# Routed layers with one block up to the experts, expert regions of fixed place, and attention operands merged with combination and normalisation

## The chip, the cores and the metric

One core of a Trainium2 chip runs one program. Its engines work side by side, each on its own instruction stream, and meet in semaphores: TensorE (PE, with its weight loads PEld), VectorE (DVE), ScalarE (ACT), GpSimd (POOL) and SyncE (SP), which issues most transfers. The metric is the device time in microseconds (us), median over runs.

## The reference

The input x has 2 x 1024 tokens of 256 values, the context 2 x 77 tokens. Four layers follow each other, each an attention and a feed-forward part with a residual sum:

```
x = x + L0_attention(norm(x), ctx);      x = x + L0_ffn(norm(x))       # causal, with mixed scores; quantised ffn
x = x + L1_attention(ctx, norm(x));      x = x + L1_ffn(norm(x))       # latent attention; ROUTED ffn, ReLU, capacity 320
x = x + L2_attention(norm(x), ctx);      x = x + L2_ffn(norm(x))       # cross attention; gated mixture of all experts
x = x + L3_attention(norm(x), ctx);      x = x + L3_ffn(norm(x))       # cross attention with a bias; ROUTED ffn, GELU, biases
```

A routed part chooses one of 8 experts for each token and computes only that one:

```
probs = softmax(norm(x) @ gate_w);  e = argmax(probs)            # per token, 8 experts
y = act(norm(x) @ w1[e] + b1[e]) @ w2[e] + b2[e]                 # 256 -> 1024 -> 256
x = x + probs[e] * y          # in L1 only for the first 320 tokens of an expert
```

A cross attention takes queries from the normalised tokens and keys and values from the context (16 heads of 16 values, 77 keys).

## The kernel before

Every stage is one or more blocks. In a block each engine has its own instruction list; a block ends when all engines have ended theirs, and the next begins. A `Stage` clears its semaphores in a block of its own when it is left. x stays in SBUF as `env.x` (16 tiles of 128 tokens), with its statistics in `env.stats`.

**Routed layer** (`routed_ffn_stage`, tags m1 and m3). `route_tokens` first issues two weight loads of 8 MB (lines 3007, 3008) and runs `layernorm_stage`: VectorE normalises 16 tiles, TensorE turns them and multiplies by the gate, ScalarE copies. A second block takes the logits of all 16 tiles at once: VectorE finds the expert of every token, TensorE counts, VectorE works out `slot`, a place in a dense list in which each expert's tokens are padded to whole tiles of 128 (`NT` = 23 tiles). GpSimd then scatters 16 tiles of rows into `sorted_x` in DRAM (line 3050, one indirect transfer a tile), which was filled with zeros in the first stage (line 754).

`routed_experts` runs over the 23 tiles. `tiles` writes out two, loops over 18, two in a turn, and writes out three. For tile j (buffer u = j % 2):

- SyncE loads the rows of a tile as soon as its buffer is free, up to two tiles ahead (line 3162).
- TensorE (`work`): `expand(j+1)`, the first product; `turn_x(j+2)`, turning of the rows; `reduce(j)`, the second product.
- VectorE: `copy_w(j+2)`, the weights of that tile's expert into `w_mine`; `keep_x(j+2)`; then the copy of the output of tile j (line 3259 or 3261).
- GpSimd stores that output to `sorted_y` (line 3170).

All engines that need the expert of a tile read its number from `expert_of` with `value_load`. TensorE and VectorE wait at the start for all weights. `combine_experts` gathers rows from `sorted_y` by `slot` (GpSimd, line 3290), VectorE adds them (3297) and takes statistics (3301).

**Cross attention** (`cross_attention_stage`, tags c2 and c3). `cross_operands` runs `layernorm_stage`, then a block of its own: loads of the weights, context turned, keys, values, the largest value over all partitions (GpSimd, line 3407), then all queries (line 3433). `cross_attend` follows.

**Latent attention** (`latent_attend`, tag lta, once for each b). For each of 16 heads and 9 key tiles TensorE scores, ScalarE takes exponentials (line 2858), VectorE and GpSimd split them into two halves, TensorE weighs. SyncE stages queries, keys and values of the next head while one is worked on.

Of the kernel before, what the change touches and what calls it, by code (L numbers as in the profile page):

```python
# [7 lines left out]
ALU = mybir.AluOpType  # L8
# [301 lines left out]
class Env:  # L310


    def __init__(self, nc, ctx):
# [8 lines left out]
        self.sorted_x = [nc.dram_tensor(f"sorted_x{k}", [NT * P, D], F32).ap() for k in range(2)]  # L322
# [4 lines left out]
        self.stored = sems("expert_rows_stored", 2)  # L327
# [343 lines left out]
def project_qkv(nc, env, st, ctx, args, name, kern_dram, q_dram, k_dram, near_dram, mixed_dram, vals, edges, size, mask, other):  # L671
# [70 lines left out]
    def _(sp):  # L742
# [1829 lines left out]
def latent_attend(nc, env, st, ctx, b, p, qT, kT, v16, v32):  # L2572
# [35 lines left out]
    TURN = 3  # L2608

# [215 lines left out]
    def _(act):  # L2825
# [20 lines left out]
        for h in range(H):  # L2846
            for j in range(KT):
# [112 lines left out]
NT = T // P + E - 1  # L2960


def routed_ffn_stage(nc, env, tag, args, name, func, biased, capacity, out=None):
# [6 lines left out]
    sorted_x, zero_stored = env.sorted_x.pop(0), env.zero_stored.pop(0)  # L2970
    sorted_y = nc.dram_tensor(f"{tag}_sorted_y", [NT * P, D], F32).ap()
    with ExitStack() as ctx:
# [5 lines left out]
        slot = st.sb("slot", [P, TILES], U32)  # L2978
        weight = st.sb("weight", [P, TILES])
        expert_of = st.sb("expert_of", [P, NT], I32)  # L2980
        weights_loaded = st.sem("weights_loaded")
        with ExitStack() as inner:
            route_tokens(nc, env, Stage(nc, inner, tag + "r"), inner, tag, w, capacity, sorted_x, zero_stored, slot, weight,
                         expert_of, w1, w2, b1, b2, weights_loaded)
        with ExitStack() as inner:
            routed_experts(nc, env, Stage(nc, inner, tag + "e"), inner, func, sorted_x, sorted_y, expert_of, w1, w2, b1, b2,
                    weights_loaded)
        with ExitStack() as inner:  # L2988
            combine_experts(nc, env, Stage(nc, inner, tag + "c"), inner, sorted_y, slot, weight, out)


def route_tokens(nc, env, st, ctx, tag, w, capacity, sorted_x, zero_stored, slot, weight, expert_of, w1, w2, b1, b2, weights_loaded):

    xn = st.sb("xn", [P, TILES, D])
    xnT = st.sb("xnT", [P, DC, T])
    gate = st.sb("gate", [P, DC, E])
    gate_loaded = st.sem("gate_loaded")
    b1_rows = st.sb("b1_rows", [E * FC, P])
    rows_loaded, b1_turned, b1_kept = (st.sem(n) for n in ("rows_loaded", "b1_turned", "b1_kept"))

    def load(sp):

        sp.dma_start(gate[:], w("gate_w").rearrange("(c p) e -> p c e", p=P)).then_inc(gate_loaded, 16)
        if b1 is not None:
            sp.dma_start(b1_rows[:], w("b1").rearrange("e (c p) -> (e c) p", p=P)).then_inc(rows_loaded, 16)
            sp.dma_start(b2[:], w("b2").partition_broadcast(P)).then_inc(weights_loaded, 16)
# [3 lines left out]
    lg_ps, lg_done = st.ps("lg_ps", [P, 512]), st.sem("lg_done")  # L3010
    layernorm_stage(nc, env, tag + "l", env.x, dst_tok=xn, dst_T=xnT, ahead=load,
                    gates=(gate, gate_loaded, 16, lg_ps, lg_done))
    upto, all_ones = st.sb("upto", [P, P], BF16), st.sb("all_ones", [P, P], BF16)
    lower = st.sb("lower", [P, E, E])
    ids = st.sb("ids", [P, E])
    tile_ids = st.sb("tile_ids", [P, NT])
# [254 lines left out]
def combine_experts(nc, env, st, ctx, sorted_y, slot, weight, out):  # L3271
# [22 lines left out]
    def _(dve):  # L3294
# [8 lines left out]
        if out is None:  # L3303
            dve.wait_ge(summed, TILES)
# [820 lines left out]
```

## Time and profile before

| | us |
|---|---|
| median of 3 runs | 3418.19 (3417.17 to 3421.18) |
| profiled execution, its own time | 3417.33 |
| its span | 3415.7 |
| TensorE / VectorE / ScalarE / GpSimd busy | 2921.4 / 2085.7 / 1895.5 / 1302.8 |
| first routed layer | about 1847 to 2080 |
| combination and operands of the second cross attention | about 2082 to 2142 |
| operands of the last attention | about 2987 to 3022 |
| second routed layer with combination | about 3152 to the end |

The span is that of the profiled execution from its first to its last instruction; stages follow each other, so a place in it names a stage. In a timeline row stand start, duration, engine, line, what is written from what, and in brackets the idle time before it with what ended it. `x16` or `x32` means that so many instructions are merged in a row.

### The profile page before, as it was taken

The numbers are of one execution on the slowest core, as the hardware profiler recorded it, in microseconds if no ns is written. First come the engines' busy times: TensorE is split into PE (matmuls) and PEld (weight loads), VectorE is DVE, ScalarE is ACT, GpSimd is POOL, SyncE is SP. The second block draws the span as 40 slices with busy tenths as digits, with TensorE's granted clock in tenths as the row PEclk, the third lists the DMA queues.
The fourth block names the chain that finished last, engine by engine and source line by source line (L and its number), as shares of the span: only waits on it lengthen the run. The fifth ranks groups of instructions, "written<-read, shape, count | busy, mean of one in ns | idle before, by whom it ended". The sixth has DMA issues, their size and how long they took to land. (4 is left out here: it accounts for less than half of the span.)

```text
span 3415.7 us, 68343 instructions
## 1 busy us (share of the span) xinstructions
PE 2921.4 (86%) x26674; PEld 2033.7 (60%) x26675; DVE 2085.7 (61%) x3098; ACT 1895.5 (55%) x2864; POOL 1302.8 (38%) x942
## 2 busy tenths in 40 slices
PE   6779998737879998889997695979999999988596
PEld 3246665415446666456666694766666666667595
DVE  6968887587867873877873224855444444466122
ACT  3448886293558884568883111755555555456131
POOL 2259998020258883157782212720000000045212
PEclk8979999878989999989997897979999999999698
DMA  4611111200022220022214311011000000042612
GB/s 147 221 56 57 54 54 57 91 13 13 1 59 53 53 47 15 16 47 58 56 38 149 114 37 45 2 31 50 26 26 26 26 26 1 1 109 62 222 37 69
DMA packets 218052, 193.21 MB, mean 57 GB/s; under 512 B 126837, under 2 KB 176865, under 8 KB 216737
## 3 DMA queue, kind: packets, MB, share of 16 engines
q1 hardware_dynamic: 210247, 172.30, 17.4%
q0 software_dynamic: 5280, 14.42, 1.3%
q8 instruction: 207, 3.39, 0.4%
q10 hardware_dynamic: 2233, 2.39, 0.2%
q14 instruction: 85, 0.70, 0.1%
HBM read 112.72 MB, written 39.00 MB: 44 GB/s over the span
## 5 line engine op out<-in xcount | busy, mean ns | idle before, releaser
L2663 POOL TENSOR_TENSOR lta_p_lo<-lta_p,lta_p_hi 128x1024 f16<-128x1024 f32 x256 | 539.0, 2133 | 218.0 <-DVE lta_p_hi L2786 218.0
L2858 ACT ACTIVATE lta_p<-lta_banks,lw_gmax 128x512 f32<-128x512 f32 x512 | 324.0, 683 | 112.7 <-PE lta_banks L2701 108.4
L2769 DVE TENSOR_REDUCE lta_s_ps<-lta_s_ps 128x1 f32<-128x1101 f32 x240 | 314.1, 1309 | 106.7 <-PE lta_s_ps L2680 106.7
L3814 PE MATMUL m_y_ps<-m_w,m_hT 128*128 128x256 f16 x3072 | 355.8, 273 | 2.4 <-DVE m_hT L3972 2.4
L3802 PE MATMUL m_h_ps<-m_x,m_w 128*128 128x512 f16 x1536 | 353.1, 380 | 3.1 <-issue 3.1
L3972 DVE TENSOR_TENSOR m_hT<-m_h,m_hT 128x512 f16<-128x512 f32 x256 | 176.9, 692 | 277.0 <-ACT m_hT L3899 275.3
L3899 ACT ACTIVATE m_h<-m_h_ps,m_h_bias,m_h_scale 128x512 f32<-128x512 f32 x256 | 199.5, 779 | 261.1 <-PE m_h_ps L3802 253.0
L3814 PEld LDWEIGHTS m_y_ps<-m_w,m_hT 128*128 128x128 f16 x3072 | 299.2, 98 | 65.4 <-issue 8.2
L1242 POOL TENSOR_TENSOR c0a_tri_p_lo<-c0a_tri_p,c0a_tri_p_hi 128x1024 f16<-128x1024 f32 (+2 forms) x192 | 285.7, 1526 | 58.2 <-DVE c0a_tri_p_hi L1416 57.4
L3802 PEld LDWEIGHTS m_h_ps<-m_x,m_w 128*128 128x128 f16 x1536 | 150.5, 98 | 159.5 <-issue 5.4
L1491 ACT ACTIVATE c0a_tri_p<-c0a_banks,c_size 128x512 f32<-128x512 f32 (+3 forms) x384 | 208.4, 577 | 45.4 <-PE c0a_banks L1310 32.6
L2700 PE MATMUL lta_banks<-lta_q,lta_k 128*128 128x512 f16 (+1 forms) x576 | 220.9, 384 | 3.2 <-ACT lta_p L2858 3.2
L3788 POOL PARTITION_ALL_REDUCE m_amax<-m_top x8 | 3.0, 376 | 571.7 <-DVE m_top L3945 571.7
L1397 DVE TENSOR_REDUCE c0a_banks<-c0a_banks 128x1 f32<-128x512 f32 (+7 forms) x256 | 190.8, 761 | 49.3 <-PE c0a_banks L1285 48.3
L2701 PE MATMUL lta_banks<-lta_q,lt_k 97*128 97x512 f16 (+1 forms) x576 | 220.4, 383 | 0.0
L3899 ACT ACTIVATE m_hT<-m_h_ps,m_h_bias,m_h_scale 128x512 f16<-128x512 f32 x256 | 199.3, 778 | 0.0
L2679 PE MATMUL lta_s_ps<-lta_k,lta_q 128*128 128x512 f16 x744 | 164.3, 330 | 40.8 <-DMA lta_k<-ltb_kT 13.8
L2786 DVE TENSOR_REDUCE lta_p_hi<-lta_p 128x1024 f16<-128x1024 f32 x128 | 155.2, 1213 | 47.3 <-ACT lta_p L2858 47.3
L2710 PE MATMUL lta_banks<-lt_vh,lta_p_hi 128*128 128x65 f16 (+1 forms) x4096 | 167.8, 193 | 0.4 <-issue 0.4
L2710 PEld LDWEIGHTS lta_banks<-lt_vh,lta_p_hi 128*128 128x128 f16 x4096 | 147.3, 97 | 13.8 <-issue 1.3
L2679 PEld LDWEIGHTS lta_s_ps<-lta_k,lta_q 128*128 128x128 f16 x744 | 59.6, 99 | 158.3 <-DVE lta_s_ps L2769 77.6
L1279 PE MATMUL c0a_banks<-c0a_tri_k,c0a_tri_q 96*128 96x512 f16 (+4 forms) x384 | 108.3, 337 | 36.5 <-DMA c0a_tri_k<-c_mixed 16.3
(760 smaller groups left out, 6582.4 us busy)
## 6 DMA issues: line engine op xcount, KB each, us to landing
m_w<-in_L_ffn_w_dram SPq DMA_DIRECT2D x4, 8192.0 KB, 40.4
m_raw<-in_L_ffn_W_dram SPq DMA_DIRECT2D x16, 1024.0 KB, 6.4
lta_q<-ltb_qT SPq DMA_DIRECT2D x96, 128.0 KB, 2.5
c_side<-in_fside_Bx16xSxS_dram SPq DMA_DIRECT2D x16, 616.0 KB, 4.7
c0a_tri_q<-c_near SPq DMA_DIRECT2D x96, 96.0 KB
c0a_tri_k<-c_mixed SPq DMA_DIRECT2D x93, 96.0 KB
lta_k<-ltb_kT SPq DMA_DIRECT2D x64, 137.6 KB, 2.6
lt_vh<-ltb_v SPq DMA_DIRECT2D x64, 128.0 KB
```

Source lines behind the costliest of these rows:

```text
L1242: nc.gpsimd.tensor_tensor(p_lo[:, slot, cols], p32[:, p32_slot(h, j), cols], p_hi[:, slot, cols], ALU.subtract).then_inc(rested, 1)
L1491: nc.scalar.activation(p32[:, slot, a:z], t_ps[:, c, at:at + z - a], ACT.Exp, scale=size[:, 0:1]).then_inc(exped, 1)
L2663: nc.gpsimd.tensor_tensor(p_lo[:, slot, :], p32[:, p32_slot(h, j), :], p_hi[:, slot, :], ALU.subtract).then_inc(rested, 1)
L2679: nc.tensor.matmul(scores(h, n)[:, cols], q11[:, u, rows], k12[:, u, cols], start=True, stop=k < 2)
L2700: nc.tensor.matmul(t_ps[0:rows, c, :], k12[:, u, keys], q11[:, u, cols], start=True, stop=False)
L2701: nc.tensor.matmul(t_ps[0:rows, c, :], k1[:, low, keys], q2[:, low, cols], start=False, stop=True).then_inc(t_done, 1)
L2710: last = nc.tensor.matmul(o_ps[:, bank, at:at + wide], weights[:, slot, n * P:(n + 1) * P], vh[:, u, j, part, 0:wide], start=len(parts) > ...
L2769: nc.vector.tensor_reduce(ntop_of(h)[:, n:n + 1], scores(h, n), AX_X, ALU.max, negate=True).then_inc(top_ready, 1)
L2858: nc.scalar.activation(p32[0:rows, slot, c * 512:(c + 1) * 512], t_ps[0:rows, c, :], ACT.Exp, bias=bias, scale=p["gmax"][0:rows, 0:1]).the ...
L3802: last = nc.tensor.matmul(h_ps[:, f % RING, :], w1[:, v, a, c, f * P:(f + 1) * P], x16[:, b, c, n * CHUNK:(n + 1) * CHUNK], start=c == 0 a ...
L3814: last = nc.tensor.matmul(y_ps[:, q, 0:D], hT[:, k % 2, a, f, q * P:(q + 1) * P], w2[:, v, b, f, :], start=f == 0 and m == 0, stop=f == FC ...
L3899: made = nc.scalar.activation(out, h_ps[:, f % RING, :], ACT.Relu, bias=h_bias[:, v, f:f + 1], scale=h_scale[:, v:v + 1])
```

## The change

- The zero fill moves from SyncE in the first stage to ScalarE in the latent attention: eight transfers of 4352 KB, four for each `sorted_x`, at heads 4, 6, 8 and 10. `sorted_x` grows from 2944 to 17408 rows: each expert has a region of 2048 rows at a fixed place, and 1024 more stay zero.
- `route_tokens` is one block: normalising, turning and gate logits go on while groups of four tiles are chosen, counted and scattered. A token's row in `sorted_x` needs only its expert and its rank there. The dense `slot` for `sorted_y` and the first row of each tile, `row_of`, are worked out behind the last group.
- Weights come in 16 transfers, w1 and w2 of one expert after the other, with a semaphore for each expert. In `routed_experts` SyncE writes a flag by a small transfer when an expert is there; TensorE and VectorE wait for `16 * e + 16`.
- The row loads go from SyncE to GpSimd, which reads `row_of` and issues `load(j+2)` ahead of the wait for the output of tile j.
- In c2 the combination, statistics, normalising, turning and queries are one block in groups of four tiles; in c3 the same without the combination. The maximum over partitions is taken by TensorE and VectorE, and `kbd` is made by GpSimd. `combine_experts` stays as it is for the last layer.

```diff
@@ latent_attend, ScalarE
+                if j == 0 and h in ZERO_AT:
+                    act.dma_start(zeros[ZERO_AT.index(h)], env.zero[:].unsqueeze(1).to_broadcast([P, SORTED_ROWS // P // ZERO_FILLS, D])
+                                  ).then_inc(env.zero_stored[b], 16)
@@ project_qkv, SyncE
-        for rows, kept in zip(env.sorted_x, env.zero_stored):
-            sp.dma_start(rows.rearrange("(j p) d -> p j d", p=P),
-                         env.zero[:].unsqueeze(1).to_broadcast([P, NT, D])).then_inc(kept, 16)
@@ route_tokens
-        sp.dma_start(w1[:], w("w1").rearrange("e (c p) f -> p e c f", p=P)).then_inc(weights_loaded, 16)
-        sp.dma_start(w2[:], w("w2").rearrange("e (c p) d -> p e c d", p=P)).then_inc(weights_loaded, 16)
+        for e in range(E):
+            sp.dma_start(w1[:, e], w("w1")[e].rearrange("(c p) f -> p c f", p=P)).then_inc(w_loaded[e], 16)
+            sp.dma_start(w2[:, e], w("w2")[e].rearrange("(c p) d -> p c d", p=P)).then_inc(w_loaded[e], 16)
...
+        for t in range(TILES):
+            if t % GROUP == 0:
+                pool.wait_ge(slot_ready, t // GROUP + 1)
+            nc.gpsimd.indirect_dma_start(sorted_x, bass.IndirectOffsetOnAxis(ap=x_slot[:, t:t + 1], axis=0),
                                          xn[:, t, :], None).then_inc(scattered, 16)
...
+        for t in range(TILES + 2):
+            if t >= 2 * GROUP and t % GROUP == 0:
+                count(t // GROUP - 2)
+            if t < TILES:
+                turn(t)
+            if t >= 2:
+                gates(t - 2)
...
+        for t in range(2 * GROUP):
+            normalise(t)
+        for g in range(groups):
+            choose(g)
+            dve.wait_ge(hot_ready, g + 1)
+            if g:
+                carry(g)
+            place_rows(g)
+            if g == 0:
+                carry(g)
+            if g + 2 < groups:
+                for t in tiles_of(g + 2):
+                    normalise(t)
@@ routed_experts
     @block.sync
-            sp.dma_start(xs[:, u, :], sorted_x[bass.ds(j * P, P), :]).then_inc(xs_loaded[u], 16)
+        for e in range(E):
+            sp.wait_ge(w_loaded[e], 32)
+            sp.dma_start(flag[0:1, e:e + 1], env.eps[0:1, 0:1]).then_inc(expert_ready, 16)
+            sp.wait_ge(expert_ready, 16 * (e + 1))
     @block.gpsimd
+        def load(j, u):
+            row = pool.value_load(row_of[0:1, bass.ds(j, 1)], min_val=0, max_val=SORTED_ROWS - P)
+            if not (isinstance(j, int) and j < 2):
+                pool.wait_ge(x_turned, j - 1)
+            nc.gpsimd.dma_start(xs[:, u, :], sorted_x[bass.ds(row, P), :]).then_inc(xs_loaded[u], 16)
+        def work(j, u):
+            if within(j, 2):
+                load(j + 2, u)
             pool.wait_ge(y_evac, j + 1)
             nc.gpsimd.dma_start(sorted_y[bass.ds(j * P, P), :], ys[:, u, :]).then_inc(ys_stored[u], 16)
+        for j in range(2):
+            load(j, j)
+        tiles(pool, work)
     reduce (TensorE) and copy_w (VectorE), after value_load:
+            pe.wait_ge(expert_ready, 16 * e + 16)
+            dve.wait_ge(expert_ready, 16 * e + 16)
@@ cross_operands, TensorE (lag is 0 in c2, 1 in c3)
+        if lag == 0:
+            context()
+        for g in range(groups):
+            for t in tiles_of(g):
+                turn(t)
+            if g == 0 and lag == 1:
+                context()
+            if g >= lag and g < groups - 1:
+                queries(g - lag)
+        if lag == 1:
+            queries(groups - 2)
+        pe.wait_ge(v_topped, 1)
+        nc.tensor.transpose(c_ps[0:1, 0:P], v_top[:], env.ident[:]).then_inc(top_turned, 1)
+        pe.wait_ge(peaked, 1)
+        nc.tensor.matmul(c_ps[:, P:P + 1], env.ones[0:1, :], peak[0:1, 0:1], start=True, stop=True).then_inc(peak_spread, 1)
+        queries(groups - 1)
@@ cross_operands, VectorE in c2
+            for g in range(groups):
+                part = slice(g * CHUNK, (g + 1) * CHUNK)
+                for t in tiles_of(g):
+                    complete(t)
+                sum_row((g + 1) * CHUNK - 1)
+                dve.wait_ge(summed, (g + 1) * CHUNK)
+                group_stats(g, part)
...
+            for t in tiles_of(groups - 1):
+                normalise(t)
+            keep_keys()
+            keep_values()
+            halve_values()
+            hide()
```

`complete(t)` is the addition of a gathered tile, with the statistics of the one before; `group_stats` is the merge chain with the root on ScalarE; `context()` is keys and values.

## Rows read from the trace of the kernel before

**Rows 1.** The page's first line, the profiled execution.
```profile
span 3415.7 us, 68343 instructions
```

**Rows 2.** Timeline, first routed layer, steady expert loop: start us, us, instruction, idle before.
```profile
1985.76 3.73 PE L3193 MATMUL m1e_h_ps<-m1e_xT,m1e_w_mine 128*128 128x128 f32 x32
1986.06 0.42 DVE L3259 COPY m1e_ys<-m1e_y_ps 128x256 f32<-128x256 f32 x1 [3.13 <-PE m1e_y_ps L3204]
1987.14 0.54 POOL L3170 DMA_DIRECT2D m_sorted_y<-m1e_ys  x1 [6.14 <-DVE m1e_ys L3259]
...
1989.33 0.38 PE L3185 MATMUL m1e_x_ps<-ident,m1e_xs 128*128 128x128 f32 x2
...
1989.55 3.62 PE L3204 MATMUL m1e_y_ps<-m_w,m1e_hT 128*128 x16
...
1993.00 3.73 PE L3193 MATMUL m1e_h_ps<-m1e_xT,m1e_w_mine 128*128 128x128 f32 x32
...
1994.15 1.23 DVE L3244 COPY m1e_w_mine<-m_w 128x2048 f32 x1 [0.43 <-issue]
1994.38 1.11 POOL L3170 DMA_DIRECT2D m_sorted_y<-m1e_ys  x1 [6.70 <-DVE m1e_ys L3259]
```

**Rows 3.** Timeline, second routed layer, steady expert loop.
```profile
3256.18 3.73 PE L3193 MATMUL m3e_h_ps<-m3e_xT,m3e_w_mine 128*128 128x128 f32 x32
3256.59 0.42 DVE L3261 TENSOR_TENSOR m3e_ys<-m3e_y_ps,m_b 128x256 f32<-128x256 f32 x1 [3.23 <-PE m3e_y_ps L3204]
...
3259.76 0.38 PE L3185 MATMUL m3e_x_ps<-ident,m3e_xs 128*128 128x128 f32 x2
```

**Rows 4.** Line 3199, reading the expert number: ns min/median/max, first and last start.
```profile
L3199 PEldq FUSED_REGOPS  x82: 37/151/166, 1915.5 to 3375.9; - x82
L3199 PEldq TENSOR_LOAD <-m_expert_of x46: 297/302/562, 1915.1 to 3375.5; - x46
```

**Rows 5.** DMA issues: KB each, median us from issue to landing.
```profile
m1e_xs<-sorted_x SPq DMA_DIRECT2D x23, 128.0 KB, 2.0
...
m_sorted_y<-m3e_ys POOLq DMA_DIRECT2D x23, 128.0 KB, 2.6
```

**Rows 6.** Second weight load (line 3008); timeline, first scatter and first product.
```profile
L3008 SPq DMA_DIRECT2D m_w<-in_L_ffn_w_dram x2: 8592/9768/10943, 1847.9 to 3153.2; - x2
...
DMA to landing us min/median/max: 54.4/54.4/54.4
...
1877.88 1.31 POOL L3050 DMA_INDIRECT sorted_x<-m1r_xn,m_slot  x1 [7.41 <-DVE m_slot L3112]
...
1906.36 6.05 PE L3193 MATMUL m1e_h_ps<-m1e_xT,m1e_w_mine 128*128 128x128 f32 x32 [0.61 <-DVE m1e_xT L3248]
```

**Rows 7.** Timeline, from the first combination to the second cross attention.
```profile
2083.65 0.97 POOL L3290 DMA_INDIRECT m1c_yg<-m_sorted_y,m_slot  x1 [0.30 <-issue]
...
2085.21 0.48 DVE L3297 SCALAR_TENSOR_TENSOR x_res<-m1c_yg,m_weight,x_res 128x256 f32<-128x256 f32 x1 [8.65 <-DMA m1c_yg<-m_sorted_y,m_slot]
2085.72 0.43 DVE L3301 BATCH_NORM_STATS2 row_stats<-x_res 128x6 f32<-128x256 f32 x1
...
2126.53 13.90 PE L3433 MATMUL c2p_q_ps<-c2p_xT,c2p_wq 128*128 128x512 f32 x32
...
2142.56 6.11 PE L3548 MATMUL c2a_s_ps<-c_kbd,c_qT 128*128 128x462 f32 x16 [2.13 <-POOL c2a_ident_b L3518]
```

**Rows 8.** Timeline, operands of the last attention.
```profile
2987.57 0.19 DVE L121 TENSOR_TENSOR c3pl_mean<-row_stats 128x16 f32<-128x16 f32 x1 [1.30 <-PEq L66]
...
2989.65 5.71 DVE L169 TENSOR_SCALAR c3pl_turn<-x_res,c3pl_mean,c3pl_rstd 128x256 f32<-128x256 f32 x16
...
3021.47 0.69 ACT L3444 ACTIVATE c_qT<-c3p_q_ps,c3p_bqs 128x512 f32<-128x512 f32 x1 [1.03 <-PE c3p_q_ps L3433]
```

**Rows 9.** Zero fills; latent attention, busy us: PE, PEld, DVE, ACT, POOL.
```profile
L754 SPq DMA_DIRECT2D sorted_x<-zero_row x2: 426/2554/4682, 66.7 to 67.2; - x2
...
1040.00:1080.00 40.00, 39.37 (x554) 26.06 (x553) 31.59 (x34) 32.38 (x46) 32.54 (x16) 1.00 0.24 51
```

More of the change, by code:

```diff
@@ L2985, in routed_ffn_stage @@
         with ExitStack() as inner:
[L2986 to L3001, printed above, removed]
+            routed_experts(nc, env, Stage(nc, inner, tag + "e"), inner, func, sorted_x, sorted_y, expert_of, row_of, w1, w2, b1, b2,
+                    w_loaded, b2_loaded)
@@ L3076, in _ @@
             nc.scalar.copy(b1[:].rearrange("p e c -> p (e c)"), b_ps[:, 0:E * FC]).then_inc(b1_kept, 1)
-            act.wait_ge(b1_kept, 1)
+        for t in range(TILES):
+            keep_rows(t)
+            if t > GROUP and t % GROUP == 2:
+                exponentials(t // GROUP - 1)
+        exponentials(groups - 1)
     @block.vector
@@ new lines, in carry @@
+        def carry(g):
+            part = slice(g * GROUP, (g + 1) * GROUP)
+            step(nc.vector.tensor_reduce(group_sum[:, g, :], hot[:, part].rearrange("p t e -> p e t"), AX_X, ALU.add))
+            if g == 0:
+                nc.vector.tensor_copy(before[:, 1, :], group_sum[:, 0, :]).then_inc(carried, 1)
+            else:
+                dve.wait_ge(carried, g)
+                nc.vector.tensor_tensor(before[:, g + 1, :], before[:, g, :], group_sum[:, g, :], ALU.add).then_inc(carried, 1)
@@ new lines, in place_rows @@
+        def place_rows(g):
+            part = slice(g * GROUP, (g + 1) * GROUP)
+            dve.wait_ge(counted, g + 1)
+            tt(place[:, part], of_group(place_ps[:, g % 2, :]), hot[:, part], ALU.mult)
+            step(nc.vector.tensor_reduce(rank[:, part], place[:, part], AX_X, ALU.add))
+            tt(base[:, part], base[:, part], rank[:, part], ALU.add)
+            nc.vector.tensor_copy(x_slot[:, part], base[:, part]).then_inc(slot_ready, 1)
+            if capacity is not None:
+                ts(fits[:, part], rank[:, part], float(capacity), None, ALU.is_le)
+                tt(weight[:, part], weight[:, part], fits[:, part], ALU.mult)
@@ L3268, in _, with combine_experts @@
         tiles(dve, work)
-def combine_experts(nc, env, st, ctx, sorted_y, slot, weight, out):
-    yg = st.sb("yg", [P, TILES, D])
-    gathered = env.gathered.pop()
-    added, stored, summed = st.sem("added"), st.sem("stored"), st.sem("summed")
-    block = ctx.enter_context(nc.Block())
-    if out is not None:
+def combine_experts(nc, env, tag, sorted_y, slot, weight, out):
+    with ExitStack() as ctx:
+        st = Stage(nc, ctx, tag)
+        yg = st.sb("yg", [P, TILES, D])
+        gathered = env.gathered.pop()
+        added, stored = st.sem("added"), st.sem("stored")
+        block = ctx.enter_context(nc.Block())
         @block.sync
@@ L3409, in _, with turn, queries @@
+        pool.wait_ge(kbd_ready, DC * B)
     @block.tensor
     def _(pe):
+        def turn(t):
+            pe.wait_ge(normed, t + 1)
+            if t >= TURNED:
+                pe.wait_ge(x_evac, t - TURNED + 1)
+            for c in range(DC):
+                last = nc.tensor.transpose(x_ps[:, t % TURNED, c * P:(c + 1) * P], rows[:, t % NORMED, c * P:(c + 1) * P],
+                                           env.ident[:])
+            last.then_inc(x_turned, 1)
+        def queries(n):
+            if n == 0:
+                pe.wait_ge(wq_loaded, 16)
+            pe.wait_ge(x_evac, CHUNK * (n + 1))
+            for f in range(DC):
+                i = DC * n + f
+                if i >= 2:
+                    pe.wait_ge(q_evac, i - 1)
+                for c in range(DC):
+                    last = nc.tensor.matmul(q_ps[:, i % 2, :], wq[:, c, f * P:(f + 1) * P], xT[:, c, n * 512:(n + 1) * 512],
+                                            start=c == 0, stop=c == DC - 1)
+                last.then_inc(q_done, 1)
```

520 lines of the change are left out of this document (332 added, 188 removed).

## Prediction

> **What bounds the kernel now.** I read the page first, then the timeline of the expert loop, then the three places where one block ends and the next begins, and last the latent attention, because the change puts new transfers there. The execution spans 3415.7 us [rows 1]. Its own time is 3417.3 us, 0.9 below the median of the runs, and the sum below is made against 3417.3.
>
> In the routed layers TensorE sets the pace. One tile of the expert loop runs: first product of tile j+1 (3.73 us), turning of tile j+2 (0.38), second product of tile j (3.62), and again; two first products start 7.24 us apart and TensorE has no gap [rows 2]. The turning finds its rows present because SyncE asked for them about two tiles ahead. Around the loops the bound is latency instead: in the first routed layer the first scatter starts at 1877.9 and the first product at 1906.4 [rows 6]; the attention after it is reached at 2142.6, 60 us after the first gather [rows 7]; the second cross attention needs from 2987.6 to 3022.2 for its operands [rows 8]. In the latent attention TensorE is busy 39.4 of 40 us and ScalarE 32.4 [rows 9].
>
> **The term that decides: row loads on GpSimd.** The loads of the tiles move from SyncE's queue to GpSimd's, since the row is now a value read from SBUF. The order there is load(2), store(0), load(3), store(1), load(4) and so on. store(j-1) waits for the output of tile j-1, so load(j+2), behind it, is issued after the second product of tile j-1. TensorE wants these rows after only one first product. A lead of two tiles becomes one of some 3.6 us.
>
> Count from S, the start of the first product that follows that second product, with S = 1985.76 [rows 2]. The output copy ends at 1986.48, S+0.72; the store starts 0.66 after it and takes 0.54, or 1.11 when VectorE's copy of the weights runs beside it: then it ends 0.11 after the copy [rows 2]. Then GpSimd reads the row (0.30), computes with it (0.15) [rows 4], waits and issues. How much of this lies under the store isn't shown. If all of it does, the load starts at once, between 1.5 and 1.9 after the output copy; between two indirect transfers GpSimd leaves 0.30 [rows 7], and with all of it in series it starts at about 2.6. I take 2.3, in the middle. From issue to landing a 128 KB transfer takes 2.0 at best, on either queue, and GpSimd's median in the second layer is 2.6 [rows 5]; I take 2.0. The rows are there 4.3 after the output copy, S+5.0. TensorE wants them at S+3.57 (1989.33) [rows 2]: 1.45 late. The second product starts 0.22 after the turning today; after a stall TensorE still has to read the expert number (0.30 and 0.15) and form the new wait, 0.4 beyond what is hidden now. That makes 1.8 a tile, times 20 tiles (loads 3 to 22) = 36. In the second routed layer the output copy ends at S+0.83 and the turning is wanted at S+3.58 [rows 3]; GpSimd collides with the weight copy more often, as the median of 2.6 shows [rows 5]: 2.1 a tile, 42. Together **+78**. The lower bound takes the earliest load and nothing after the turning: 0.65 and 0.75, +28; the upper takes all in series and a landing of 2.6: 2.8 a tile, +112. A gain is excluded, as TensorE's own work is the same.
>
> The Trainium skill (DMA: Bandwidth & Descriptors, Anatomy of one DMA) fits a transfer from GpSimd as 2.0 us plus its bytes over 436 GB/s, which is 2.3 for 128 KB. The best rows here show 2.0; by the page the sum would be 12 us higher.
>
> **The attention after the first routed layer.** Gather, addition, statistics, normalising, turning and queries become one block. The gathers keep their pace of 1.27 (0.97 and 0.30) [rows 7]; their start moves 0.5 later behind two small GpSimd steps. Per group of four tiles VectorE does four additions and four statistics (0.48 and 0.43 each, with gaps 3.9) and a merge chain, today 2.1 from its first step to the first normalising [rows 7, 8], plus a shift: 6.2. The first row is added at 2085.7, group 0 follows the gathers and is through at 2092.8, the last at 2092.8 + 3 x 6.2 = 2111.4. Then come four normalisings (0.36 each [rows 8]), keys, values and their maximum (some 2.2), the maximum across partitions over TensorE (0.9): 2115.9. Two of the eight query products are held behind it, 13.90 / 4 = 3.5 [rows 7], up to twice that at the 1.2 GHz level, since TensorE idles much here; I add half. The copy and the next block need 2.1. The attention starts near 2123.3, not 2142.6: **-19** (bounds -15 and -22). The four key products that move to GpSimd lie beside values and queries; uncovered they would cost about 3, which is why the lower end is 15.
>
> **The operands of the last attention.** Weights are asked for at the block's start and TensorE no longer pauses. Its work in series: turning 5.7 [rows 8], queries 13.9 [rows 7], the maximum 0.9, and the context: 8 products of 154 columns and 8 of 256, which by the queries' 0.43 for 512 columns (13.90 / 32) take 2.8 at 2.4 GHz and 5.6 at 1.2; I take 5.2, because TensorE comes out of a pause, and 0.5 for turning. Together 26.2, from about 2990.2 (the first normalising at 2989.65 and a step). With the last copy it ends at 3017.2, against 3022.2: **-5** (bounds -3 and -8).
>
> **Routing.** Choosing, counting and scattering by groups of four tiles lets the first scatter go at about 1860 and not 1877.9 [rows 6], an estimate: eight normalisings, four turnings and about fourteen VectorE steps of 0.2. Each later group costs about 7.7, so the last scatter lands near 1892 and not 1902. But the expert weights land 54.4 after their issue at 1847.9, that is 1902.3, and 3153.2 + 54.4 = 3207.6 in the second layer [rows 6]. The experts now wait for a flag per expert, written by a small transfer which SyncE issues behind all sixteen weight transfers on the same queue. If it travels behind them, it lands no sooner than they do. Then the copy of the weights (1.23) can start at 1902.8 and the first product at 1904.1, 2.3 earlier than 1906.36; the same in the second layer: **-4.5**. If the flag doesn't queue, about 9 each, -18; no gain at all is the other bound. Sixteen smaller loads carry the same bytes.
>
> That an engine of the queue takes descriptors in ring order is what the Trainium skill says (DMA: Bandwidth & Descriptors, Queues, rings and completion order); no run here shows it for a flag. Without the rule I would give this term -9 and the sum would fall by 4.5.
>
> **Zero fills.** Two fills of 2944 KB leave the first stage: the second held SyncE 4.68 us [rows 9], while nobody waited; 0. Eight fills of 4352 KB are now issued by ScalarE inside the latent attention. A first transfer on an idle queue held its issuer 0.43 [rows 9], and ScalarE has 7.6 of 40 us free, so **+1**. If each held ScalarE as the second fill did SyncE, 8 x 4.7 = +37: the upper bound. Loads of queries and keys there are asked for a head ahead and hide the shared bandwidth.
>
> **Sum:** 78 - 19 - 5 - 4.5 + 1 = +50.5, so 3417.3 + 50.5 = 3467.8, say 3468: slower by 1.5%.
>
> **Rivals.** (1) *The loads are early enough*, the side on which the change gains: GpSimd issues them under the store or the expert loop keeps its 7.24. Then -27.5 is left, 3390. It is decided where the rows land 2.85 us after the output copy; against it stands that the store alone starts 0.66 after that copy and a landing takes 2.0. Chance 0.12. (2) *The stall is at its lower bound* and the gains at their upper ones: 28 - 22 - 8 - 10 = -12, 3405, up to no change; 0.09. (3) *Fills hold ScalarE* in the latent attention, TensorE waits for exponentials: 3468 + 36 = 3504. For it, the 4.68; against it, the 50 us between fills on their own queue. 0.09. (4) *The granted clock falls in the loops*, as TensorE now idles a fifth of the time. The first product takes 6.05 at the start, and 3.73 later [rows 2, 6]; 2.3 a tile in 46 tiles is +107, 3575. Busy stretches today show the full clock; 0.05. (5) *The change does what it says*, no load waits, and the experts start early as well: -41, 3377; 0.03.
>
> My forecast keeps 0.62. **How the numbers follow.** With the bounds of its terms it reaches from about 3425 to 3500. The range 3410 to 3504 leaves out (1), (4), (5) and part of (2). Within 0.2% (6.8 us, about what a measurement of this kernel can tell from no change) lies only the upper part of (2), 0.05. Faster: (1), (5) and the rest of (2), 0.19. Slower 0.76.
>
> **What would show it.** In the profile after: turning in the expert loop waits for a transfer some 1.4 us in 20 tiles of each layer, and first products start 9.0 and 9.3 us apart; the first product of the layer starts near 1904; the attention starts 19 us sooner after the first gather; the latent attention lasts as long as now. The prediction is wrong if the period stays 7.24, or if ScalarE shows gaps of microseconds at its eight fills.

## The result, and the profile after

The changed kernel takes 3512.5 us (median of 4 runs, 3509.3 to 3516.7) against 3417.7 for the kernel before on the same chip: ratio 1.0278, 95% interval 1.026 to 1.0296. It is slower by 95 us; the forecast was 3468, slower by 51, with a range up to 3504. The profiled executions have spans of 3514.1 and 3415.7 us.

The table splits both spans at the same events. All times are differences of starts in the timelines, save that the last product of the latent output is taken at its end; the end of a loop is the start of its last output copy.

| stretch, us | before | after | difference | forecast |
|---|---|---|---|---|
| start to the last product of the latent output | 1843.8 | 1849.6 | +5.8 | +1 |
| to the first product of the first expert loop | 62.6 | 58.8 | -3.8 | -2.3 |
| first expert loop | 169.8 | 228.3 | +58.5 | +36 |
| loop end to first gather | 6.2 | 8.7 | +2.5 | +0.5, counted within the -19 |
| first gather to the second cross attention | 60.2 | 44.6 | -15.6 | -19 |
| to the last attention's first product | 881.1 | 873.6 | -7.5 | -5 |
| to the first product of the second expert loop | 188.7 | 185.2 | -3.5 | -2.3 |
| second expert loop | 170.5 | 231.0 | +60.5 | +42 |
| loop end to first gather | 6.4 | 8.5 | +2.1 | 0 |

The two loops add 119 us and everything else together takes 20 off, which makes the 99 of the table; the spans differ by 98.4, the medians by 95. Here is the first loop of the changed kernel in its timeline (start, duration, engine, line, tiles, idle time before it and what ended it), at about the place of [rows 2]:

```profile
1983.79 3.73 PE L3309 MATMUL m1e_h_ps<-m1e_xT,m1e_w_mine 128*128 128x128 f32 x32
1984.09 0.43 DVE L3377 COPY m1e_ys<-m1e_y_ps 128x256 f32<-128x256 f32 x1 [4.08 <-PE m1e_y_ps L3321]
1985.30 1.13 POOL L3286 DMA_DIRECT2D m_sorted_y<-m1e_ys  x1 [8.06 <-DVE m1e_ys L3377]
1986.54 0.54 POOL L3280 DMA_DIRECT2D m1e_xs<-sorted_x  x1
1988.91 0.44 PE L3301 MATMUL m1e_x_ps<-ident,m1e_xs 128*128 128x128 f32 x2 [1.38 <-DMA m1e_xs<-sorted_x]
1990.05 3.72 PE L3321 MATMUL m1e_y_ps<-m_w,m1e_hT 128*128 x16 [0.70 <-issue]
1993.60 3.73 PE L3309 MATMUL m1e_h_ps<-m1e_xT,m1e_w_mine 128*128 128x128 f32 x32
...
1999.09 0.44 PE L3301 MATMUL m1e_x_ps<-ident,m1e_xs 128*128 128x128 f32 x2 [1.75 <-DMA m1e_xs<-sorted_x]
2000.26 3.71 PE L3321 MATMUL m1e_y_ps<-m_w,m1e_hT 128*128 x16 [0.74 <-issue]
```

Two first products are 9.81 and 10.22 us apart instead of 7.24. GpSimd's row load stands directly behind its store, and the turning waits for it. The second product then starts 1.14 to 1.17 after the turning, where [rows 2] have 0.22. From there a third thing adds to it in some tiles. These are TensorE's rows a little later, and the view by windows (busy time of each engine, then PEclk, the granted clock of TensorE) of a second product as usual and of the one at 2020.27:

```profile
2019.13 0.44 PE L3301 MATMUL m1e_x_ps<-ident,m1e_xs 128*128 128x128 f32 x2 [1.77 <-DMA m1e_xs<-sorted_x]
2020.27 5.11 PE L3321 MATMUL m1e_y_ps<-m_w,m1e_hT 128*128 x16 [0.70 <-issue]
```

```profile
1990.05:1993.60 3.55, 3.55 (x16) 3.14 (x17) 0.00 (x0) 0.00 (x0) 0.00 (x0) 1.00 0.00 0
2020.27:2025.22 4.95, 4.95 (x16) 4.16 (x17) 0.00 (x0) 0.00 (x0) 0.00 (x0) 0.71 0.00 0
2020.00:2022.00 2.00, 1.73 (x4) 1.47 (x5) 0.04 (x1) 0.00 (x0) 0.00 (x0) 0.50 0.00 0
```

The same sixteen matmuls take 1.4 us more; the granted clock is 0.50, that is 1.2 GHz, in their first two microseconds. Such a period (above 11 us) comes 3 times in the first loop and 5 times in the second; in the kernel before every period of the steady loops is 7.24 or 7.25.

At the head of the first routed layer the rows answer to [rows 6]:

```profile
1866.20 1.31 POOL L3056 DMA_INDIRECT sorted_x<-m1r_xn,m1r_x_slot  x1 [12.28 <-DVE m1r_x_slot L3188]
...
1897.55 13.99 SPq L3271 DMA_DIRECT2D m1e_flag<-eps  x5
...
1904.24 0.69 PE L3301 MATMUL m1e_x_ps<-ident,m1e_xs 128*128 128x128 f32 x2 [19.79 <-DMA m1e_xs<-sorted_x]
...
1906.65 1.23 DVE L3362 COPY m1e_w_mine<-m_w 128x2048 f32 x1 [15.84 <-DMA m1e_flag<-eps]
...
1908.36 3.96 PE L3309 MATMUL m1e_h_ps<-m1e_xT,m1e_w_mine 128*128 128x128 f32 x17 [3.44 <-DVE m1e_xT L3366]
```

The layer's block starts 5.7 us later than before, so the first scatter, some 12 us earlier in the span, is 17 us earlier in the layer; yet the first product gains only 3.8, because the copy of the weights waits for a flag of a few bytes that SyncE issued at 1897.55 and that landed 9 us later. It came with the last weights, which were issued at 1893.51 and took 13.3 us, so until 1906.8, though both weight transfers of the first expert had landed by 1862.1. That agrees with the rule of the Trainium skill (DMA: Bandwidth & Descriptors, Queues, rings and completion order) that a DMA engine takes the descriptors of a queue in ring order. The shared bandwidth alone explains less: the 128 KB of rows that GpSimd issued at 1898.87, beside the same weights, landed in 5.3 us.

At the combination and the second cross attention (compare [rows 7]):

```profile
2137.39 0.54 POOL L3286 DMA_DIRECT2D m_sorted_y<-m1e_ys  x1 [2.91 <-DVE m1e_ys L3377]
...
2144.53 0.10 POOL L3525 MEMSET c2p_ind<- 128x8 f32 x1 [6.60 <-POOLq L66]
...
2145.37 1.04 POOL L3531 DMA_INDIRECT c2p_yg<-m_sorted_y,slot  x1 [0.47 <-issue]
...
2156.84 0.17 DVE L121 TENSOR_TENSOR c2p_mean<-row_stats 128x4 f32<-128x4 f32 x1
...
2178.82 1.38 DVE L3678 TENSOR_SCALAR c2p_rows<-x_res,c2p_mean,c2p_rstd 128x256 f32<-128x256 f32 x4
...
2189.98 4.42 PE L3816 MATMUL c2a_s_ps<-c_kbd,c_qT 128*128 128x462 f32 x9 [2.27 <-POOL c2a_ident_b L3786]
```

The merged block does shorten the way to the attention, from 60.2 to 44.6. The first two rows show something that the forecast had not: GpSimd is idle for 6.60 us between its last store and the next block, where it was idle for 4.93 in the kernel before.

The operands of the last attention, from the first statistics step to the first product (compare [rows 8]; in the kernel before that product is at 3023.7):

```profile
3032.94 0.20 DVE L121 TENSOR_TENSOR c3p_mean<-row_stats 128x16 f32<-128x16 f32 x1
...
3063.53 0.66 PE L3816 MATMUL c3a_s_ps<-c_kbd,c_qT 128*128 128x462 f32 x1 [2.47 <-POOL c3a_ident_b L3786]
```

### The profile page after: what moved, and what is told of

The parts are those of the page before. It is cut to its first block and busy times, and to the rows that moved or that the text cites. A ratio compares the mean times of both kernels' runs of the same rounds, so it can differ in the third digit from the quotient of the medians.

```text
span 3514.1 us, 68707 instructions
## 1 busy us (share of the span) xinstructions
PE 2961.7 (84%) x26656; PEld 2044.4 (58%) x26657; DVE 2101.1 (60%) x3243; ACT 1902.1 (54%) x2887; POOL 1345.7 (38%) x991
## 5 line engine op out<-in xcount | busy, mean ns | idle before, releaser
L1239 POOL TENSOR_TENSOR c0a_tri_p_lo<-c0a_tri_p,c0a_tri_p_hi 128x1024 f16<-128x1024 f32 (+2 forms) x192 | 285.7, 1523 | 58.8 <-DVE c0a_tri_p_hi L1413 57.7
L3348 ACT ACTIVATE m3e_hT<-m3e_h_ps,m_b 128x128 f32<-128x128 f32 x184 | 50.1, 383 | 185.8 <-PE m3e_h_ps L3309 185.8
```

What stands on the lines that cost most here:

```text
L1239: nc.gpsimd.tensor_tensor(p_lo[:, slot, cols], p32[:, p32_slot(h, j), cols], p_hi[:, slot, cols], ALU.subtract).then_inc(rested, 1)
```

## The experiments

**One tile more of lead.** If the row loads only come too late in GpSimd's queue, one edit must give nearly everything back.

```diff
 def work(j, u):                       # GpSimd
-    if within(j, 2):
-        load(j + 2, u)
+    if within(j, 3):
+        load(j + 3, 1 - u)
     pool.wait_ge(y_evac, j + 1)
...
-for j in range(2):
-    load(j, j)
+for j in range(3):
+    load(j, j % 2)
```

> The changed kernel with one edit: GpSimd asks for the rows of tile j+3 ahead of the wait for output j, instead of those of tile j+2. Theory (the loads come too late in GpSimd's queue): first products of the expert loops stand 7.2 to 7.5 us apart again, not 9.8 to 10.2, the turning waits for nothing, the second product never takes 5 us (the granted clock no longer falls), and some 115 us of the 119 that the two loops gained are gone: 3395 to 3405. Rival A (the reading of the expert's number and the wait against a register cost TensorE 0.5 us a tile whether the rows are there or not): period 7.7, 3415 to 3425. Rival B (the loops are slow because GpSimd's queue itself is too slow, value read, load and store in series): period stays above 9, above 3480.

Measured: 3385.3 us (3382.9 to 3391.9), ratio to the kernel before 0.990 (0.989 to 0.992): 127 us less than the changed kernel, and faster than the kernel before. It is also 10 us below the expected range, which had counted on some 115 us; in the traces the loops alone are 121 shorter, and what gave the other 6 is open. Its timeline:

```profile
1985.58 3.73 PE L3309 MATMUL m1e_h_ps<-m1e_xT,m1e_w_mine 128*128 128x128 f32 x32
...
1987.00 1.56 POOL L3286 DMA_DIRECT2D m_sorted_y<-m1e_ys  x1 [5.44 <-DVE m1e_ys L3377]
...
1988.77 0.54 POOL L3280 DMA_DIRECT2D m1e_xs<-sorted_x  x1 [0.21 <-issue]
1989.15 0.38 PE L3301 MATMUL m1e_x_ps<-ident,m1e_xs 128*128 128x128 f32 x2
...
1989.37 3.62 PE L3321 MATMUL m1e_y_ps<-m_w,m1e_hT 128*128 x16
```

The load still stands behind the store and starts even later, but the turning at 1989.15 wants another, older load. The period is 7.24 in all tiles but the first two, the loops take 169.0 and 169.2 us, and no second product of the steady part takes longer than 3.62 us. The value read, the wait against a register in every tile and the slower queue cost TensorE nothing once the rows are there: rivals A and B fall.

**The order alone, on the kernel before.** Here nothing of the change is in but the late loads: fixed rows, no value read by GpSimd, no flags.

```diff
 # before: SyncE's loads are taken out, GpSimd's work becomes
 def store(j, u):
+    if within(j, 2):
+        load(j + 2, u)
     pool.wait_ge(y_evac, j + 1)
     nc.gpsimd.dma_start(sorted_y[bass.ds(j * P, P), :], ys[:, u, :]).then_inc(ys_stored[u], 16)
```

> The kernel before with one edit: GpSimd issues the row loads, load(j+2) behind store(j-1) and ahead of the wait for output j, from the same fixed rows as before (no value is read, no wait against a register, no flag). It takes from the change only the queue and the order. Theory (order alone makes the loss): first products 9.3 to 9.8 us apart, turning waits 1.0 to 1.6 us for the load, 3417 + 2 x 45 to 55 = 3505 to 3530. Rival A (the value read on GpSimd, 0.45 us, and the wait of TensorE against a register make a good part): period 8.5 to 9.0, 3475 to 3495. Rival B (queue and order cost nothing by themselves): 3417.

Measured: 3544.2 us (3543.6 to 3547.1), ratio 1.037 (1.035 to 1.039), 126 us more than before, and above the range that was expected. Loops 228.2 and 225.9. Its timeline, a usual tile and a slow one:

```profile
1986.71 0.44 PE L3190 MATMUL m1e_x_ps<-ident,m1e_xs 128*128 128x128 f32 x2 [1.06 <-DMA m1e_xs<-sorted_x]
...
1987.76 3.72 PE L3209 MATMUL m1e_y_ps<-m_w,m1e_hT 128*128 x16 [0.61 <-issue]
...
1996.69 0.44 PE L3190 MATMUL m1e_x_ps<-ident,m1e_xs 128*128 128x128 f32 x2 [1.64 <-DMA m1e_xs<-sorted_x]
...
1997.77 5.40 PE L3209 MATMUL m1e_y_ps<-m_w,m1e_hT 128*128 x16 [0.64 <-issue]
```

The undisturbed periods are 9.5 and 10.0, shorter than the 9.8 and 10.2 of the changed kernel by 0.2 to 0.3: without the value read the load starts 0.26 and 0.14 sooner after the output copy, and without the wait against a register the second product starts some 0.1 sooner after the turning. But 12 of 40 periods are above 11 us, not 8. How many there are is partly chance: e4_small_fills below, with the loops of the changed kernel, has 10. The two loops lose 58.4 and 55.4 us here, 114 of the 126, against 119 in the changed kernel, so the queue and the order make nearly all of the loops' loss. The other 12 us lie outside the loops: 4.0 at the two loop ends, 6.5 in the two long stretches between the second cross attention and the second expert loop, which the edit does not touch, and 2 ahead of the first expert loop. In the two stretches the granted clock is 0.96 and 0.79, where it was 0.97 and 0.81; what makes the 6.5 stays open.

**The late order without GpSimd.** SyncE issues the loads of the kernel before, but only after the output of the tile three before has been copied, the moment from which GpSimd begins its store.

```diff
 def load(j, u):                       # SyncE, tiles 0 to 2 as before
-    sp.wait_ge(x_turned, j - 1)
+    sp.wait_ge(y_evac, j - 2)
```

> The kernel before with one edit: SyncE, not GpSimd, issues the row loads, and only when the output of the tile three before has been copied, the moment from which GpSimd starts its store and then the load in the changed kernel. It keeps the late order and takes away the store and GpSimd's own time ahead of the load. Theory (the loop stalls by the time by which the rows land more than 2.9 to 3.0 us after the output copy, and no further): the load is issued 0.1 to 0.3 after the copy and lands 2.0 to 2.6 later, which is just in time: period 7.24 to 7.5, 3417 to 3430. Rival (any lead below a tile costs, because the load collides with the store): 8 to 8.5, 3450 to 3475.

Measured: 3434.9 us (3428.2 to 3437.8), ratio 1.005 (1.003 to 1.006), just above what the theory gave. Its timeline:

```profile
1987.04 3.73 PE L3201 MATMUL m1e_h_ps<-m1e_xT,m1e_w_mine 128*128 128x128 f32 x32
1987.35 0.43 DVE L3267 COPY m1e_ys<-m1e_y_ps 128x256 f32<-128x256 f32 x1 [3.56 <-PE m1e_y_ps L3212]
1987.95 15.59 SPq L3164 DMA_DIRECT2D m1e_xs<-sorted_x  x3
...
1990.61 0.38 PE L3193 MATMUL m1e_x_ps<-ident,m1e_xs 128*128 128x128 f32 x2
...
1991.08 3.72 PE L3212 MATMUL m1e_y_ps<-m_w,m1e_hT 128*128 x16
```

The load is issued 0.17 after the copy (1987.78) and lands 2.0 later by the median of its line, so at about 1989.95. The turning is not late: it starts 3.57 after the first product, as in [rows 2]. Nevertheless the second product starts 0.47 after it, and not 0.22, and the period is 7.25 to 7.7. From the landing to the second product it is 1.13 us; in the changed kernel, where the turning starts when the rows land, 1.14 to 1.17. So the second product follows the landing by no less than some 1.1 us. The read of the expert's number on TensorE's own instruction stream shows why. These are the rows of that read (ns min/median/max, first and last start) in one tile of the kernel before, of the changed kernel and of this one:

```profile
L3199 PEldq TENSOR_LOAD <-m_expert_of x1: 298/298/298, 1987.7 to 1987.7; - x1
```

```profile
L3315 PEldq TENSOR_LOAD <-m_expert_of x1: 297/297/297, 1989.0 to 1989.0; - x1
```

```profile
L3207 PEldq TENSOR_LOAD <-m_expert_of x1: 298/298/298, 1990.1 to 1990.1; - x1
```

In the kernel before the read starts 1.6 us ahead of the turning (1989.33). In the changed kernel it starts 0.1 after it (1988.91), and here it starts as the rows land, ahead of a turning at 1990.61. In nearly all steady tiles of the changed kernel, of e5_before_late and of this one it comes 0.14 us after the landing, and the second product 0.85 to 1.2 us after the read. The wait for the rows stands ahead of the read in TensorE's list and holds it up. The rows have to be there some 0.9 us before the turning is due (1.13 less 0.22), not merely on time: in the tiles of the first loop whose rows landed 0.84 to 0.99 ahead, the second product is 0.22 to 0.25 behind the turning.

**The flags.** Three runs on top of e1_early. The first takes the flags out and waits once for all weights; the second sets them by GpSimd; the third does so ahead of the load of the third tile.

```diff
 # GpSimd, e3_early_poolflag              SyncE's eight flag transfers are gone
+for e in range(E):
+    pool.wait_ge(w_loaded[e], 32)
+    nc.gpsimd.memset(flag[0:1, e:e + 1], 0.0).then_inc(expert_ready, 1)
 # e9_flags_first: the same loop, but between load(1) and load(2)
 # TensorE and VectorE wait for e + 1 and not for 16 * e + 16
```

> As e1_early, and without the flags: TensorE and VectorE wait once at the start for all sixteen weight transfers, and not in each tile against a register. Theory (late loads are all): loops as in e1_early within 3 us a layer; the first product starts at about the same time as in e1_early or some 1 to 2 us earlier, because the flag of the first expert landed only when all weights had. Rival A: period 7.24 here and 7.7 in e1_early, 20 us less than there. If flags did let the experts start early, this run is slower at the first product by some us.

> As e1_early, but an expert's flag is no longer a transfer: GpSimd waits for the expert's two weight transfers and adds to the semaphore with a memset of one value. Theory (the flag was held behind the weights in the queue that it shares with them): the first weights are there long before, so the first product of each layer starts when its rows and the copy of its weights are there, 4 to 6 us sooner than in e1_early, 8 to 12 us less in all. Rival (the weights themselves were late): the first product starts no sooner, within 2 us of e1_early. GpSimd can't store before all weights are in, but the first output comes later than that.

> As e3_early_poolflag, but GpSimd sets the eight flags ahead of its load of the third tile. In e3_early_poolflag that load waited for the first turning, and the first copy of the weights behind it until 1901.07, when seven flags came at once. Theory (an expert's weights are there long before the last of them, and only the flag was late): the copy of the weights starts at the block's start, the first product right after the first rows (landed at 1899.2 there) are turned and copied, at some 56 us after the latent attention's last product instead of 58.4: 2 to 3 us less than e3_early_poolflag in the first routed layer and about as much in the second, 3380 to 3382. Rival (rows and weights share the transfers' bandwidth and the rows come later now): no change, 3385.

Measured, in this order: 3388.8 (3387.1 to 3398.6), 3386.0 (3383.0 to 3391.5) and 3381.6 (3378.8 to 3384.6), against 3385.3 for e1_early. The ranges of the first two overlap with that of e1_early (3382.9 to 3391.9), so what each is worth is read from the stretches. From the latent attention's output to the first product it is 59.8, 58.5 and 56.0 us, against 57.9; from the last attention to the second layer's first product 187.8, 184.7 and 182.2, against 185.4. So the flag transfers are worth some 2 us a layer over waiting for all weights, and the first version of GpSimd's flags nothing clear of these differences, where 8 to 12 had been expected. Its trace shows why:

```profile
1899.20 0.69 PE L3301 MATMUL m1e_x_ps<-ident,m1e_xs 128*128 128x128 f32 x2 [19.76 <-DMA m1e_xs<-sorted_x]
1900.54 0.54 POOL L3277 DMA_DIRECT2D m1e_xs<-sorted_x  x1 [4.90 <-PE m1e_x_ps L3301]
1901.07 0.26 POOL L3289 MEMSET m1e_flag<- 1x1 f32 x7
1901.31 1.23 DVE L3362 COPY m1e_w_mine<-m_w 128x2048 f32 x1 [15.52 <-POOL m1e_flag L3289]
```

The flags stood behind the load of the third tile, which waits for the first turning. In e9_flags_first they don't:

```profile
1894.48 0.26 POOL L3289 MEMSET m1e_flag<- 1x1 f32 x7
1894.72 1.23 DVE L3363 COPY m1e_w_mine<-m_w 128x2048 f32 x1 [10.10 <-POOL m1e_flag L3289]
1898.09 0.69 PE L3302 MATMUL m1e_x_ps<-ident,m1e_xs 128*128 128x128 f32 x2 [19.82 <-DMA m1e_xs<-sorted_x]
```

At 1894.48 seven experts' weights are there, so the weights were not late, the flag was. With 3381.6 the time came out in the expected 3380 to 3382. What is left to wait for is the first load of rows, issued at 1892.75 and landed some 5 us later amid the last weights.

**The zero fills.** The changed kernel with 11.3 MB of zeros instead of 34.8: 384 rows of each expert's region in the first layer, 768 in the second, and the last 1024 rows, in nine transfers of ScalarE a batch instead of four.

```diff
-    ZERO_AT = (4, 6, 8, 10)
-    zeros = env.sorted_x[b].rearrange("(k j p) d -> k p j d", p=P, k=ZERO_FILLS)
+    ZERO_AT = tuple(range(3, 3 + ZERO_FILLS))                 # ZERO_FILLS = E + 1
+    starts = [(e * T, FILLED[b]) for e in range(E)] + [(E * T, E * P)]     # FILLED = 384, 768
```

> The changed kernel, with zero fills only of the rows that are read: 384 or 768 rows of each expert's region and the last 1024, nine transfers a batch of 0.4 to 1 MB each instead of four of 4.35 MB (11.3 MB in all, not 34.8). ScalarE issues more transfers than before the edit. Theory (the fills took bandwidth from the staging of queries and keys in the latent attention): the first routed layer starts 4 to 6 us sooner, near its place in the kernel before, 3507. Rival (issuing them holds ScalarE): no sooner, or 1 to 3 us later, 3512 to 3516. Second rival (the 5.7 us are of another kind, the code or the clock): no change.

Measured: 3509.0 us (3506.3 to 3511.1), 3.5 less than the changed kernel, with ranges that overlap. The view by windows over 359 us of the second batch's latent attention, for the changed kernel and for this one (the last three numbers are granted clock, share and GB/s of the transfers):

```profile
1453.00:1812.00 359.00, 338.44 (x4542) 217.09 (x4540) 265.86 (x269) 271.80 (x383) 269.57 (x128) 0.97 0.39 98
```

```profile
1453.00:1812.00 359.00, 336.49 (x4543) 217.49 (x4544) 262.53 (x270) 273.02 (x385) 269.45 (x128) 0.97 0.29 67
```

With the large fills the transfers move half as much again in this stretch, and from its first to its last product the attention lasts 360.0 us with them, 359.8 in this kernel and 359.8 in the kernel before. The latent output does end 8.0 us sooner than in the changed kernel, at 1841.6, which the expectation had as the sign of its theory, and the first loop is 4.1 us longer (232.4, with a period of 13.2 us among its slow ones), which hides it in the total. But the theory falls all the same: the 5.8 us at the head of the table do not come from the fills. They lie in two stretches that the change does not touch, between the two attentions (145.3 us before, 148.5 after) and in the output product (34.8 and 36.8). The same stretches are 145.5 and 34.9 in this kernel and in e3_early_poolflag, whose fills are those of the changed kernel; they are 148.5 and 36.9 in e7_best below, which has the small ones, and 148.1 and 36.9 in e6_merged below, which has those of the kernel before. It differs from one profiled kernel to the next, with no regard to the fills; what sets it stays open.

**The merged operands alone**, on the kernel before.

```diff
 # kernel before, with combine_experts, cross_attention_stage and cross_operands of the changed kernel;
 # route_tokens, routed_experts, the loads and the zero fills as before
```

> The kernel before with only the merged operand blocks of the second cross attention and of the last attention; routing, expert loops and zero fills as before. Theory: the second cross attention is reached 15 us sooner after the first gather (46 and not 62) and the last one 6 us sooner: 3396. Forecast of the prediction: 19 and 5, 3393. Rival (what looked like a gain in these blocks is given back behind them): 3405 to 3417.

Measured: 3392.2 us (3391.3 to 3395.2), ratio 0.992 (0.991 to 0.994): 26 us faster than the kernel before, 1 below the 3393 of the prediction. From the first gather to the second cross attention it is 44.1 us, and from there to the last attention's first product 872.4, so 16.1 and 8.7 us less.

**All repairs together, and SyncE again.** e7_best has the longer lead, flags by GpSimd in their first, held-up place, and the small fills. e11_sync_loads has the full fills and the flags first, and GpSimd issues no row load at all.

```diff
 # e11_sync_loads, SyncE (ScalarE issues tiles 0 and 1)
+def load(j, u):
+    row = sp.value_load(row_of[0:1, bass.ds(j, 1)], min_val=0, max_val=SORTED_ROWS - P)
+    sp.wait_ge(x_turned, j - 1)
+    sp.dma_start(xs[:, u, :], sorted_x[bass.ds(row, P), :]).then_inc(xs_loaded[u], 16)
```

> The changed kernel with three edits together: rows asked for a tile earlier, flags by GpSimd instead of by transfers, and the small zero fills. Theory: the gains of the merged blocks (15 and 6), of routing (4 before the edit, and 8 to 12 more by the flags) stay, the loops are as in the kernel before: 3417 - 21 - 12 to 16 = 3380 to 3386, faster than the kernel before by 1%. Rival (waits against registers cost 0.5 us a tile): 3400 to 3405. Rival (the parts take time from one another): above 3417.

> The changed kernel with the flags set by GpSimd first, the first two row loads by ScalarE and all others by SyncE, which reads the row and keeps two tiles of lead; GpSimd only stores, as in the kernel before. Theory (whenever GpSimd issued row loads, the step from the last output product to the first gather took 8.4 to 8.8 us instead of 6.2 to 6.6): that step is 6.2 to 6.6 again in both routed layers, 4 us less than e9_flags_first: 3376 to 3378. Rival (the step got longer by the number of semaphores that are cleared, or by code): 8.7 remains and the time is that of e9_flags_first.

Measured: 3388.0 (3383.1 to 3391.4) and 3381.0 (3375.3 to 3383.1), ratio 0.989 (0.987 to 0.990) for the latter. e7_best is no better than e1_early (3385.3) and above the expected 3380 to 3386: its two further edits together show no gain. In e11_sync_loads GpSimd's pause ahead of the next block is shorter than in the changed kernel, 5.06 and not 6.60:

```profile
2072.97 0.54 POOL L3282 DMA_DIRECT2D m_sorted_y<-m1e_ys  x1 [2.91 <-DVE m1e_ys L3377]
2078.57 0.11 POOL L3525 MEMSET c2p_ind<- 128x8 f32 x1 [5.06 <-POOLq L66]
```

The step from loop end to gather is 7.2 and 6.6 us, against 8.7 and 8.5 in e9_flags_first. That is 3.4 us less in two places, but the medians differ by 0.6 only and their ranges overlap: shown for the step, not for the time, for which 3376 to 3378 had been expected. The first step is still 0.6 above the 6.6 of e6_merged, which has the same block behind it, so not all of its growth is explained. The two kernels are the fastest of all, 1.0 to 1.1% ahead of the kernel before.

## Why the prediction was right and wrong

**The sign and its reason were right.** The row loads on GpSimd, behind the store of the tile before, make the loss; queue and order put on the kernel before cost 126 us (114 in the loops), and one tile more of lead gives 127 back. The rival that the loads are early enough fell. The medians also add up, with the late loads priced on the kernel before: 3417.7 - 26 (merged operands) - 7 (routing and flags, e1_early against e6_merged) + 126 = 3511, where 3512.5 was measured.

**The step that failed is the size of the expert loops**, +78 forecast and +119 measured, above even its stated upper bound of +112. The mechanism was the right one; the term for a tile was a lateness and what follows it, with the clock at nothing:

- *The turning is late*, forecast 1.45 and 1.7 in the second layer: the two tiles shown start it 5.12 and 5.49 after the first product, 1.55 and 1.92 late. GpSimd starts the load 2.0 and 2.4 after the output copy, around the 2.3 assumed; the rows were taken to land 2.0 after, and they took 2.4 to the turning (the median from issue to landing is 2.3). The fit of the Trainium skill (DMA: Bandwidth & Descriptors, Anatomy of one DMA), 2.3 us for 128 KB, agrees with this median; the forecast had put it aside for SyncE's best rows, at 12 us in the sum. In the second layer the lateness was as forecast, so this is about 5 us in all.
- *What follows the turning*, forecast +0.4: it is +0.93 (1.14 to 1.17 instead of 0.22). This was the largest error, 0.53 x 40 = 21 us. The forecast priced the read of the expert's number; the whole way from that read to the second product, some 1.0 us, came behind the landing of the rows. Little of it is the wait against a register: e5_before_late has none and still shows 0.95 to 1.08 in nearly all tiles. By the same token the bound of rival (1), rows landing 2.85 us after the output copy, was too generous: in e10_sync_late they land some 2.2 after it, and 14 us are lost in the two loops.
- *The granted clock*, forecast nothing, with a rival that it falls everywhere: it falls in 3 + 5 of 40 tiles, about 1.5 us each, 12 us. That is neither the forecast nor the rival at 3575, but a small part of the rival, which belonged into the sum.

The second product itself takes 3.72 us instead of 3.62 in the other tiles (compare the rows at 1990.05 with [rows 2]), 4 us in all. For the first loop: 20 x (1.67 + 0.93 + 0.1) + 3 x 1.5 = 58.5, which is what was measured. The errors are 5, 21, 12 and 4 us, and make up the 41 that were missing.

**The gains** came as argued. Second cross attention -15.6 for -19: the first group's merge began 11.5 us after the first gather and ended its chain at 13.5, where 10.5 had been taken, and each further group took 6.7 instead of 6.2. Last attention: 36.1 us from its first statistics step to its first product before, 30.6 after, -5.5 for -5. Routing -3.8 and -3.5 for -2.3 each: the flag that comes only with the last weights was the right mechanism, and e9_flags_first shows the other branch of the forecast, a flag that doesn't queue: -6.6 and -6.5 for the -9 each that it gave, as the first rows become the bound.

**Missing from the forecast**: 2.5 and 2.1 us at the two loop ends, and 4.8 of the 5.8 us ahead of the first routed layer, whose cause stays open. **Rightly small**: the zero fills, +1 forecast; the second batch's latent attention lasts 0.2 us longer with them. The upper bound of +37 for them fell.

## What to carry to other kernels

When a load is put into a queue that also holds a wait for the result of the work which the load feeds, its lead is what lies between that wait and the use, not the number of buffers; count it in microseconds from the wait, with issue and landing, and ask for the data one tile earlier if it is short. Price the stall of an engine whose list goes on only behind the wait as more than the wait: here the register read and the waits behind it, which had been hidden behind work, added 0.93 us a tile to a stall of 1.7, and the clock fell in the same place in some tiles. A signal sent on the queue that carries the data can wait for data that it has nothing to do with: here the first expert's flag came with the last expert's weights.

## What the runs showed that was not expected

- A wait that ended before TensorE was idle still cost time: with rows landing about 0.7 us before the turning was due (e10_sync_late), the turning started on time and the product behind it 0.25 us late in the tile shown.
- With idle times of 1.4 to 1.8 and 0.7 us in every tile the granted clock fell to 1.2 GHz in a tile now and then (8 of 40 in the changed kernel, 10 of 40 in e4_small_fills with the same loops, and 12 of 40 in e5_before_late with slightly shorter ones), while most tiles stayed at 2.4 GHz.
- When GpSimd issued row loads, the step from the loop's last output copy to the next block's first gather took 8.2 to 8.7 us in eight kernels, and 6.2 to 7.2 in the four in which it only stored. The loads had landed many microseconds before; why the block ends later stays open.
